# Switch layer of a two-layer ViT tower: 16 experts on every token, against one expert per tile of sorted tokens moved by indirect DMA

## Chip, cores and metric

The program runs on one core of one Trainium2 chip. The metric is the device time of the whole program in microseconds (us), from the first to the last instruction with what lies around it; lower is better. Engines: PE (TensorE, with PEld its weight loads), DVE (VectorE), ACT (ScalarE), POOL (GpSimd), SP (SyncE, which only issues DMAs here).

## What is computed

16 images of 32x32 tokens with 29 features go through two layers, all in float32. S = 1024 tokens of C = 128 features per image.

- Layer 0: tokens are embedded and get a position table; group norm; attention with 8 heads of 64; residual; a causal MLP over features.
- Layer 1: attention with 8 heads of 16, then the switch layer, which is what changes here.

```python
logits = z @ switch_w.T + switch_b                  # z [16, 1024, 128], 16 experts
p, e = max(softmax(logits)), argmax(logits)         # one expert per token
pos = number of earlier tokens (of all images, in order) that chose e
y = z @ expert_w[e].T + expert_b[e]
out = h + (p * y if pos < CAP else p * z)           # CAP = int(1.2 * 16384 / 16)
```

Only one expert's product is used for a token.

## The kernel before

**Order.** Each image passes through segments. In a segment of kind `loop` the core works on three images at once: layer 0 of image i+2 (`seg.l0`), layer 1 of image i+1 (`seg.l1`) and the switch layer of image i (`seg.sw`); the embedding of image i+3 (`seg.nxt`) goes on beside them. The kinds are `first` (layer 0 alone, 208 steps), `second` (both layers, but no switch layer yet), `loop` (13 passes of a hardware loop), `penult` (no embedding) and `final` (layer 1 and a switch layer, 128 steps). `second`, `loop` and `penult` have 256 steps: 32 units (a half of the queries of one head of one layer) of 8 steps, one step for each 128 keys. A layer-0 unit and a layer-1 unit alternate from unit 4 to 27 (`units_of`, L29).

**Steps.** Every engine has its own instruction list, written out by hand in the order of the steps. In a step PE computes one tile of scores (L909 and L911, or L911 alone for layer 1) and one tile of a pass that looks for row maxima (`max_tile`, L883); DVE reduces the latter (L1643), ACT takes the exponential (L1144). Both have two banks, so PE can be two steps ahead. For layer 0 the probabilities are split in two bf16 parts and POOL makes the low part (`lo_parts`, L508), four instructions per unit, at kt 2, 4, 6 and at kt 0 of the next unit. In kt 2, 3, 5, 6 PE multiplies the previous unit's probabilities with the values (L927, L934, or L949 and L959). Row maxima reach the score stacks by a small DMA (`row`, L600): 8 steps before the unit that needs them, 4 steps before it in `final`. SP also loads head stacks (`load_stack`, L603).

**Everything else** is laid between the steps by tables of steps (`switch_slots`, `embed_slots`, `mlp_slots` and others, L141 to 210). A generator on each engine yields the step at which its next piece is due (`Beside`, L306). Such pieces share two PSUM banks, the glue banks, in an order that `glue_plan` (L216) derives from the same tables; `await_filled` and `await_drained` wait on them.

**The switch layer** (`switch`, on PE L827, ACT L1109, POOL L1284, DVE L1558) makes the logits, the one-hot choice `oh` and the rank in its image (`prefix`, added up by POOL, L1292), weights `wgt` and `kr` (0 over capacity), adds `un * z` and the biases to the residual `hm`, and then computes all 16 experts for each of the 8 token tiles: 32 matmuls of 128x512 (L869) against the weights `ewT`, resident in SBUF, in 16 rounds of two, and on DVE 128 multiply-adds (L1633) of a column of `wgt`. Rounds are due at the starts of units 8 to 23 (steps 64 to 185). SP stores `hm` at step 191 (L662). In `final` one switch layer is computed beside the steps, and the last image's follows after them with nothing beside it (prefix `f.`, L1014, L1726): this is called the tail.

## Time and profile before

| | us |
|---|---|
| median of 3 runs (6678.85 to 6692.49) | 6685.7 |
| the profiled execution, its own time | 6688.62 |
| its span in the trace | 6686.8 |
| granted clock of TensorE, mean (1 is 2.4 GHz) | 0.951 |

In the profile an engine's busy time is the time that its instructions cover; `x` is a count. A float32 matmul leaves two records for one instruction; the score tiles, whose type is a rounded float32, leave one. Idle time is put in front of the instruction that ended it, with its releaser. DMAs are listed with the time from issue to landing. The segments begin, by the ACT exponentials that count the steps, at 387.5 (`second`), 743.4 (the loop, about 404 a pass), 5989.6 (`penult`) and 6382.5 (`final`); the last step ends at 6565.

### The profile page before, as it was taken

To read this page: it belongs to the slowest core of one execution; us is meant where nothing else is said; L and a number is where in the kernel's file an instruction comes from. 1 tells how busy PE (TensorE), PEld (TensorE's weight loads), DVE (VectorE), ACT (ScalarE), POOL (GpSimd) and SP (SyncE) were. 2 spreads that over 40 slices of the span, in tenths; PEclk is the share of its full clock that TensorE was granted. 3 is DMA by queue.
4 is the path that set the end of the run, shared out by engine and by line. 5 is a ranking of instruction groups with operands and counts; after the bars stand their busy time and mean duration, and the time that the engine had idled before them with its cause. 6 is when DMAs were issued, how large, how long until landed. Compare 5 with 4: busy or idle time off the path is not lost.

```text
span 6686.8 us, 127962 instructions
## 1 busy us (share of the span) xinstructions
PE 6054.2 (91%) x40167; PEld 4030.8 (60%) x40167; DVE 4525.2 (68%) x11162; ACT 3211.2 (48%) x6321; POOL 2464.2 (37%) x2215
## 2 busy tenths in 40 slices
PE   6889898998989999898998989999899998999986
PEld 4556665666666666665666656666665666666643
DVE  4466676776767767676766767767676676767664
ACT  2345545454455544545445444444455445454541
POOL 2534333433333343333433333333333333333300
PEclk7899999999999999999999999999999999999997
DMA  2131221222122121221211222121221212212110
GB/s 60 42 68 42 59 52 44 52 49 50 42 53 49 40 54 42 60 49 32 64 46 47 49 56 49 40 50 46 55 45 41 61 34 60 52 47 45 30 30 9
DMA packets 98049, 317.05 MB, mean 47 GB/s; under 512 B 27782, under 2 KB 32854, under 8 KB 87126
## 3 DMA queue, kind: packets, MB, share of 16 engines
q1 hardware_dynamic: 97366, 308.41, 19.9%
q8 instruction: 371, 6.08, 0.4%
q14 instruction: 312, 2.56, 0.1%
HBM read 57.19 MB, written 41.94 MB: 15 GB/s over the span
## 4 chain that ended last, share of the span: by engine, by line
issue 47%; POOL 27%; PE 16%; DVE 6%; DMA 1%; POOLq 1%; ACT 1%; SPq 1%; DVEq 0%; ACTq 0%
POOL pr_lo L508 22%; PE bank L883 3%; POOL on L1267 3%; PE bank L911 2%; PE bank L869 2%; DVE mxh L1643 2%; PE bank L949 2%; DVE z L1431 1%; DMA stacks<-parts 1%; PE bank L934 1%; PE bank L927 1%; POOL rs L1238 1%; PE bank L793 1%; PE bank L909 1%; PE bank L959 1%
## 5 line engine op out<-in xcount | busy, mean ns | idle before, releaser
L1643 DVE TENSOR_REDUCE mxh<-bank 128x1 f32<-128x512 f32 x4096 | 2790.7, 687 | 1663.0 <-PE bank L883 1636.9
L1144 ACT ACTIVATE pr<-bank 128x512 f32<-128x512 f32 x4096 | 2419.1, 597 | 2658.8 <-PE bank L911 2613.9
L883 PE MATMUL bank<-stacks 128*128 128x512 f32 x4096 | 2224.3, 544 | 340.9 <-DVE mxh L1643 232.9
L508 POOL TENSOR_TENSOR pr_lo<-pr 128x1024 bf16<-128x1024 f32 x960 | 1823.5, 1900 | 1165.4 <-ACT pr L1144 1165.3
L911 PE MATMUL bank<-stacks 65*128 65x512 f32 (+1 forms) x4096 | 1662.0, 406 | 5.0 <-ACT pr L1144 5.0
L883 PEld LDWEIGHTS bank<-stacks 128*128 128x128 f32 x4096 | 800.8, 196 | 1132.8 <-DVE mxh L1643 809.4
L1267 POOL TENSOR_TENSOR on<-on,o_r 128x128 f32<-128x128 f32 x512 | 235.0, 459 | 1967.6 <-DVE on L1673 1967.5
L911 PEld LDWEIGHTS bank<-stacks 65*128 65x128 f32 (+1 forms) x4096 | 798.7, 195 | 223.6 <-ACT pr L1144 62.0
L909 PE MATMUL bank<-stacks 128*128 128x512 f32 x2048 | 833.5, 407 | 0.2 <-ACT pr L1144 0.2
L869 PE MATMUL bank<-ewT,mx 128*128 128x512 f32 x1024 | 589.0, 662 | 113.9 <-DVE hm L1633 44.8
L927 PE MATMUL bank<-v,pr 128*128 128x129 bf16 x8192 | 654.9, 223 | 0.8 <-ACT pr L1144 0.8
L934 PE MATMUL bank<-v,pr_lo 128*128 128x129 bf16 x8192 | 650.0, 221 | 4.2 <-POOL pr_lo L508 2.5
L927 PEld LDWEIGHTS bank<-v,pr 128*128 128x128 bf16 x8192 | 476.4, 99 | 283.7 <-issue 269.2
L1633 DVE SCALAR_TENSOR_TENSOR hm<-bank,wgt,hm 128x128 f32<-128x128 f32 x2048 | 570.6, 342 | 51.5 <-PE bank L869 51.5
L949 PE MATMUL bank<-pr,v 128*32 128x512 f32 x4096 | 547.0, 609 | 0.0
L934 PEld LDWEIGHTS bank<-v,pr_lo 128*128 128x128 bf16 x8192 | 517.4, 98 | 11.3 <-POOL pr_lo L508 10.3
L909 PEld LDWEIGHTS bank<-stacks 128*128 128x128 f32 x2048 | 403.9, 197 | 132.8 <-ACT pr L1144 77.5
L869 PEld LDWEIGHTS bank<-ewT,mx 128*128 128x128 f32 x1024 | 186.0, 204 | 237.1 <-DVE hm L1633 69.0
L959 PEld LDWEIGHTS bank<-fold,oT 128*128 128x128 f32 x2048 | 267.1, 196 | 59.5 <-ACT oT L1161 46.4
L1044 ACT ACTIVATE parts<-bank,cols 128x512 fp32r<-128x512 f32 x256 | 176.1, 688 | 233.4 <-PE bank L721 232.6
L959 PE MATMUL bank<-fold,oT 128*128 128x32 f32 x2048 | 260.5, 271 | 12.5 <-ACT oT L1161 12.5
L1275 POOL TENSOR_TENSOR on<-on,o_r 128x64 f32<-128x64 f32 x256 | 75.1, 293 | 515.1 <-DVE on L1685 515.0
(171 smaller groups left out, 5072.4 us busy)
## 6 DMA issues: line engine op xcount, KB each, us to landing
stacks<-parts SPq DMA_DIRECT2D x384, 512.0 KB, 6.5
stacks<-parts_d SPq DMA_DIRECT2D x224, 128.0 KB, 3.0
parts_d<-mx SPq DMA_DIRECT2D x16, 1024.0 KB, 4.6
stacks<-parts_d SPq DMA_DIRECT2D x224, 64.0 KB, 2.8
stage<-in_pe SPq DMA_DIRECT2D x16, 512.0 KB, 8.1
stacks<-mrow SPq DMA_DIRECT2D x512, 2.0 KB
parts_d<-on SPq DMA_DIRECT2D x16, 512.0 KB, 5.3
parts_d<-stage SPq DMA_DIRECT2D x16, 512.0 KB, 6.2
```

Of the source, the lines that this page charges most:

```text
L508: return eng.tensor_tensor(low_of(u, kt - 1).rearrange("p a b -> p (a b)"), w, hi, ALU.subtract)
L869: mm(bank[:, :], mT[:, t * P:(t + 1) * P], ewT[:, 4 * q:4 * q + 4, :].rearrange("p e f -> p (e f)"), start=True, stop=True).then_inc(fille ...
L883: mm(maxb[k % 2][:, :], qs[:, t * P:(t + 1) * P], ks[:, g * HALF:(g + 1) * HALF], start=True, stop=True).then_inc(max_filled.sem, 1)
L909: mm(bank[:, :], kA[:, head % 2, kk], qA[:, head % 2, q], start=True, stop=False)
L911: mm(bank[:, :], k_stack(layer, head)[0:last, kk], q_stack(layer, head)[0:last, q], start=(layer == 1), stop=True).then_inc(score_filled.s ...
L927: mm(dst, hi, v0[:, head // 2 % 2, kt, head % 2, 0:w], start=(kt == 0), stop=False)
L934: last = mm(dst, lo, v0[:, head // 2 % 2, kt, head % 2, 0:w], start=False, stop=(kt == T - 1))
L949: last = mm(obank[n % 2][QUAD * r:QUAD * (r + 1), :], v1[:, kt, col:col + QUAD], pr[:, at % 2, kt, :], start=(j == 0), stop=(j == 1))
L959: last = mm(obank[n % 2][:, QUAD * t:QUAD * (t + 1)], oT[:, t * P:(t + 1) * P], fold[:, :], start=True, stop=True)
L1144: act.activation(pr[:, at % 2, kt, :], score[k % 2][:, :], ACT.Exp, scale=SCALES[layer]).then_inc(exp_done.sem, 1)
L1633: ins = dve.scalar_tensor_tensor(hm[:, t, :], bank[:, e * P:(e + 1) * P], wgt[:, t, 4 * q + e:4 * q + e + 1], hm[:, t, :], ALU.mult, ALU.add)
L1643: dve.tensor_reduce(mxh[:, layer, n // 2, n % 2:n % 2 + 1], maxb[k % 2][:, :], AX_X, ALU.max)\
```

## The change

Step 64 to 185's rounds go. In their place:

- DVE builds tables (`tables`, from step 46, 10 instructions and a copy): how many tiles of 128 slots each expert needs in this image, where each expert's slots begin, and the expert of each of 24 tiles. At `place` it adds a slot number per token (4 more instructions).
- POOL scatters the 8 token tiles of `z` by 8 indirect DMAs into `x_sort_d` in DRAM (two a step from step 65), each row at its slot.
- SP loads the sorted tokens in 6 groups of 4 tiles (256 KB each, step 76, then from 86 every 12 steps), reads the expert numbers from SBUF into a register 24 times and loads each tile's 64 KB of weights from `ew_d` in DRAM, two groups ahead, and stores each group's result. In a group the order is: load of the next group, wait for this group's product, four reads and weight loads, store.
- PE transposes 4 tiles (`slots`, step 83 + 12g), ACT moves them, PE multiplies 4 tiles (`product`, 85 + 12g), DVE copies the result out (one step later).
- POOL gathers 8 tiles of results by 8 indirect DMAs (two a step from step 160); DVE adds `kr * y` in 8 instructions (from step 170, after waiting for all gathers). `hm` is stored at step 176.
- In `final` the steps are: `tables` 23, scatter 35, groups from 48 every 10, gather 112, sum 122; in the tail all of it runs in order.
- At the start SP stores the turned weights (1 MB) and three times 512 KB of zeros to DRAM, ahead of the first load of x.

```diff
-        at = {"oT1.0": 1, "oT1.1": 2, "attn1.0": 5, "attn1.1": 6, "ln.0": 7, "ln.1": 8, "z.0": 9, "z.1": 10, "zT3.0": 11, "zT3.1": 13, "logits": 15,
-              "route": 16, "rank": 21, "place": 24, "wT0": 29, "wT1": 30, "eb0": 32, "eb1": 33}
-        first = [37 + 16 * m + s for m in range(6) for s in (0, 3, 8)][:16]
+        at = {"oT1.0": 1, "oT1.1": 2, "attn1.0": 5, "attn1.1": 6, "ln.0": 7, "ln.1": 8, "z.0": 9, "z.1": 10, "zT3.0": 11, "zT3.1": 13,
+              "logits": 15, "route": 16, "rank": 21, "tables": 23, "place": 28, "wT0": 33, "wT1": 34, "eb0": 36, "eb1": 37,
+              "scatter": 35}
+        group, period, sums = 48, 10, (112, 122)
     else:
         at = {"oT1.0": 18, "oT1.1": 19, "attn1.0": 21, "attn1.1": 22, "ln.0": 22, "ln.1": 24, "z.0": 26, "z.1": 28, "zT3.0": 30, "zT3.1": 31,
-              "logits": 36, "route": 38, "rank": 44, "place": 54, "wT0": 59, "wT1": 60, "eb0": 62, "eb1": 63}
-        first = [8 * m for m in range(8, 24)]
-    return {**at, **{f"e{n}.{d}": s + d for n, s in enumerate(first) for d in range(2)}}
-
-
-NO_BANK = ("route", "place", "copy", "res0", "gn", "xn", *(f"{name}.{g}" for name in ("ln", "z", "ln1", "z1", "ln2", "z2") for g in range(2)))
+              "logits": 36, "route": 38, "rank": 44, "tables": 46, "place": 54, "wT0": 59, "wT1": 60, "eb0": 62, "eb1": 63, "scatter": 65}
+        group, period, sums = 80, 12, (160, 170)
+    at.update({f"{name}{g}": group + period * g + step for g in range(GROUPS)
+               for name, step in (("load", 6 - period if g else -4), ("slots", 3), ("product", 5), ("weights", 7), ("store", 7))})
+    return {**at, "gather": sums[0], "sum": sums[1]}
...
+        x_sort, y_sort, y_own = z[:, 0:4, :], z[:, 4:8, :], mT.rearrange("p (t c) -> p t c", t=T)
...
+            def store_prep():
+                sp.dma_start(ew_d.rearrange("e d f -> d e f"), ewT).then_inc(prep_out, 16)
+                for n in range(3):
+                    sp.dma_start(x_sort_d[n * S:(n + 1) * S, :].rearrange("(t p) c -> p t c", p=P),
+                                 stacks1[:, n % 2, 1, :].rearrange("p (t c) -> p t c", t=T).bitcast(F32)).then_inc(prep_out, 16)
...
+            def switch(seg, pre, b):
+                AT = switch_slots(seg.kind)
+                def load_weights(g):
+                    for j in range(4 * g, 4 * g + 4):
+                        e = sp.value_load(tile_ei[0:1, j:j + 1], min_val=0, max_val=E - 1)
+                        sp.dma_start(wring[:, j % 8, :], ew_d[e]).then_inc(weights_in[g % 2].sem, 16)
+                for g in range(2):
+                    yield AT["tables"] + 4 + 2 * g
+                    if g == 0:
+                        await_all((tiles_ready.sem, tiles_ready.at(b, 1)))
+                        sp.nop(nofuse=True)
+                    load_weights(g)
+                def load_slots(g):
+                    sp.dma_start(x_sort, x_sort_d[4 * g * P:4 * (g + 1) * P, :].rearrange("(t p) c -> p t c", p=P))\
+                        .then_inc(x_sort_in.sem, 16)
+                yield AT["load0"]
+                await_all((scattered.sem, scattered.at(b, 16 * T)))
+                load_slots(0)
+                for g in range(GROUPS):
+                    if g + 1 < GROUPS:
+                        yield AT[f"load{g + 1}"]
+                        await_all(drained(seg, f"{pre}slots{g}"))
+                        load_slots(g + 1)
+                    yield AT[f"weights{g}"]
+                    await_all(drained(seg, f"{pre}product{g}"))
+                    if g + 2 < GROUPS:
+                        sp.nop(nofuse=True)
+                        load_weights(g + 2)
+                    yield AT[f"store{g}"]
+                    sp.dma_start(y_sort_d[4 * g * P:4 * (g + 1) * P, :].rearrange("(t p) c -> p t c", p=P), y_sort)\
+                        .then_inc(y_sort_out.sem, 16)
...
-                        await_drained(sp, seg, "e15.1")
+                        await_all((hm_ready.sem, hm_ready.at(seg.sw, 1)))
...
-                for n in range(16):
-                    for d in range(2):
-                        yield AT[f"e{n}.{d}"]
-                        t, q = 2 * (n // 4) + d, n % 4
-                        bank, filled = use(seg, f"{pre}e{n}.{d}")
-                        mm(bank[:, :], mT[:, t * P:(t + 1) * P], ewT[:, 4 * q:4 * q + 4, :].rearrange("p e f -> p (e f)"),
-                           start=True, stop=True).then_inc(filled, 1)
+                for g in range(GROUPS):
+                    yield AT[f"slots{g}"]
+                    te.wait_ge(x_sort_in.sem, x_sort_in.at(b, 16 * (g + 1)))
+                    turn(seg, f"{pre}slots{g}", lambda j: x_sort[:, j, :])
+                    yield AT[f"product{g}"]
+                    te.wait_ge(weights_in[g % 2].sem, weights_in[g % 2].at(b, 64 * (g // 2 + 1)))
+                    bank, filled = use(seg, f"{pre}product{g}", f"{pre}slots{g}")
+                    for j in range(4):
+                        at = g % 2 * HALF + j * P
+                        last = mm(bank[:, j * P:(j + 1) * P], mT[:, at:at + P], wring[:, (4 * g + j) % 8, :], start=True, stop=True)
+                    last.then_inc(filled, 1)
...
+                    if name == "oT0.2.0" and seg.sw:
+                        act.wait_ge(y_sort_out.sem, y_sort_out.at(seg.sw, 16 * GROUPS))
...
+                    move_T(seg, f"{pre}slots{g}", half(mT, g % 2))
...
+                for t in range(T):
+                    if t % 2 == 0:
+                        yield AT["scatter"] + t // 2
+                    if t == 0:
+                        pool.wait_ge(slot_ready.sem, slot_ready.at(b, 1))
+                        pool.nop(nofuse=True)
+                    pool.indirect_dma_start(x_sort_d, bass.IndirectOffsetOnAxis(slot_i[:, t:t + 1], 0), z[:, t, :], None)\
+                        .then_inc(scattered.sem, 16)
+                for t in range(T):
+                    if t % 2 == 0:
+                        yield AT["gather"] + t // 2
+                    if t == 0:
+                        pool.wait_ge(y_sort_out.sem, y_sort_out.at(b, 16 * GROUPS))
+                        pool.nop(nofuse=True)
+                    pool.indirect_dma_start(y_own[:, t, :], None, y_sort_d, bass.IndirectOffsetOnAxis(slot_i[:, t:t + 1], 0))\
+                        .then_inc(y_own_in.sem, 16)
...
-                link(seg, dve.tensor_tensor(prefix[:, 0, :], bank[:, 0:E], seen[:, :], ALU.add))
-                dve.tensor_tensor(seen[:, :], bank[:, E:2 * E], seen[:, :], ALU.add).then_inc(drained, 1)
+                mark(seg, dve.tensor_tensor(prefix[:, 0, :], bank[:, 0:E], seen[:, :], ALU.add))
+                dve.tensor_copy(own, bank[:, E:2 * E]).then_inc(drained, 1)
+                yield AT["tables"]
+                await_drained(dve, seg, f"{pre}rank")
+                over = tile_of[:, 0:T, :].rearrange("p t e -> p (t e)").rearrange("p (e t) -> p e t", t=T)
+                link(seg, dve.tensor_tensor(over, own.unsqueeze(2).broadcast_to([P, E, T]),
+                                            steps_128[:, :].unsqueeze(1).broadcast_to([P, E, T]), ALU.is_gt))
+                link(seg, dve.tensor_reduce(tiles, over, AX_X, ALU.add))
+                yield AT["tables"] + 1
+                below = tile_of[:, 0:E, :]
+                link(seg, dve.tensor_tensor(below, tiles.unsqueeze(1).broadcast_to([P, E, E]), earlier[:, :, :], ALU.mult))
+                link(seg, dve.tensor_reduce(begin, below, AX_X, ALU.add))
+                yield AT["tables"] + 2
+                mark(seg, dve.tensor_tensor(tiles, tiles, begin, ALU.add))
+                link(seg, dve.scalar_tensor_tensor(shift, begin, float(P), seen[:, :], ALU.mult, ALU.subtract))
+                mark(seg, dve.tensor_tensor(seen[:, :], own, seen[:, :], ALU.add))
+                link(seg, dve.tensor_tensor(tile_of[:, :, :], tiles.unsqueeze(1).broadcast_to([P, TILES, E]),
+                                            tile_no[:, :].unsqueeze(2).broadcast_to([P, TILES, E]), ALU.is_le))
+                yield AT["tables"] + 3
+                link(seg, dve.tensor_reduce(tile_e[:, :], tile_of[:, :, :], AX_X, ALU.add))
+                dve.tensor_scalar(tile_ei[:, :], tile_e[:, :], float(E - 1), None, ALU.min).then_inc(tiles_ready.sem, 1)
...
+                yield AT["place"] + 2
+                link(seg, dve.tensor_tensor(lg[:, :, :], oh[:, :, :], shift.unsqueeze(1).broadcast_to([P, T, E]), ALU.mult))
+                link(seg, dve.tensor_reduce(slot[:, :], lg[:, :, :], AX_X, ALU.add))
+                link(seg, dve.tensor_tensor(slot[:, :], slot[:, :], pos, ALU.add))
+                mark(seg, dve.tensor_copy(slot_i[:, :], slot[:, :]))
                 for t in range(T):
                     if t % 4 == 0:
-                        yield AT["place"] + 2 + t // 4
+                        yield AT["place"] + 3 + t // 4
                     ins = dve.scalar_tensor_tensor(hm[:, t, :], z[:, t, :], un[:, t:t + 1], hm[:, t, :], ALU.mult, ALU.add)
-                    if t % 4 == 3:
+                    if t == 3:
                         mark(seg, ins)
-                settle(seg)
+                link(seg, ins)
+                dve.sem_inc(slot_ready.sem, 1)
                 for g in range(2):
                     yield AT[f"eb{g}"]
                     add_result(seg, f"{pre}eb{g}", g, hm, hm)
-
-                for n in range(16):
-                    yield AT[f"e{n}.1"] + 1
-                    if n == 0:
+                for g in range(GROUPS):
+                    yield AT[f"product{g}"] + 1
+                    bank, drained = await_filled(dve, seg, f"{pre}product{g}")
+                    if g > 0:
+                        dve.wait_ge(y_sort_out.sem, y_sort_out.at(b, 16 * g))
+                    dve.tensor_copy(y_sort, bank_tiles(bank)).then_inc(drained, 1)
+                for t in range(T):
+                    if t % 2 == 0:
+                        yield AT["sum"] + t // 2
+                    if t == 0:
+                        dve.wait_ge(y_own_in.sem, y_own_in.at(b, 16 * T))
                         await_drained(dve, seg, f"{pre}eb0", f"{pre}eb1")
-                    elif n % 4 > 0:
-                        await_drained(dve, seg, f"{pre}e{n - 1}.0", f"{pre}e{n - 1}.1")
-                    both = [await_filled(dve, seg, f"{pre}e{n}.{d}") for d in range(2)]
-                    q = n % 4
-                    for e in range(4):
-                        if e == 2:
-                            yield AT[f"e{n}.1"] + 2
-                        for d, (bank, drained) in enumerate(both):
-                            t = 2 * (n // 4) + d
-                            if e > 0:
-                                settle(seg, 0 if (e, d) == (3, 1) else 1)
-                            ins = dve.scalar_tensor_tensor(hm[:, t, :], bank[:, e * P:(e + 1) * P],
-                                                           wgt[:, t, 4 * q + e:4 * q + e + 1], hm[:, t, :], ALU.mult, ALU.add)
-                            if e == 3:
-                                ins.then_inc(drained, 1)
-                            else:
-                                mark(seg, ins)
+                    ins = dve.scalar_tensor_tensor(hm[:, t, :], y_own[:, t, :], kr[:, t:t + 1], hm[:, t, :], ALU.mult, ALU.add)
+                ins.then_inc(hm_ready.sem, 1)
...
-STORE_STEPS = {"loop": 191, "penult": 191, "final": 124}
+STORE_STEPS = {"loop": 176, "penult": 176, "final": 126}
```

## Rows read from the trace of the kernel before

**Rows 1.** The profile's page: span, busy time of each engine.
```profile
...
span 6686.8 us, 127962 instructions
...
PE 6054.2 (91%) x40167; PEld 4030.8 (60%) x40167; DVE 4525.2 (68%) x11162; ACT 3211.2 (48%) x6321; POOL 2464.2 (37%) x2215
...
```

**Rows 2.** Busy us of each engine in five stretches (window, length, engines, clock, DMA).
```profile
core 0: us, PE busy (x) PEld busy (x) DVE busy (x) ACT busy (x) POOL busy (x), PEclk, DMA share, GB/s
482.71:639.47 156.76, 150.62 (x1109) 100.67 (x1107) 102.48 (x222) 88.06 (x183) 71.27 (x61) 1.00 0.24 55
627.04:639.47 12.43, 10.93 (x61) 6.77 (x60) 11.14 (x37) 5.61 (x13) 8.40 (x8) 1.00 0.11 32
3272.61:3459.29 186.68, 179.15 (x1173) 115.29 (x1172) 135.91 (x353) 88.55 (x182) 70.34 (x59) 0.97 0.22 49
3439.11:3459.29 20.18, 16.85 (x65) 9.50 (x64) 12.79 (x47) 5.67 (x13) 8.54 (x8) 0.75 0.14 47
6095.52:6271.08 175.56, 172.24 (x1146) 110.95 (x1145) 130.38 (x328) 87.03 (x179) 67.86 (x55) 0.99 0.21 49
```

**Rows 3.** Groups of the stretch 3272.61 to 3459.29, by line.
```profile
...
L1643 DVE TENSOR_REDUCE mxh<-bank 128x1 f32<-128x512 f32 x128 | 88.1, 688 | 45.5 <-PE bank L883 45.0
...
L508 POOL TENSOR_TENSOR pr_lo<-pr 128x1024 bf16<-128x1024 f32 x32 | 60.7, 1898 | 40.4 <-ACT pr L1144 40.4
...
L1633 DVE SCALAR_TENSOR_TENSOR hm<-bank,wgt,hm 128x128 f32<-128x128 f32 x128 | 35.7, 342 | 0.0
L869 PE MATMUL bank<-ewT,mx 128*128 128x512 f32 x64 | 35.4, 636 | 5.1 <-DVE parts L1443 1.9 <-DVE stage L1438 1.7 <-DVE v L1455 1.1
...
```

**Rows 4.** Timeline of PE, three places: start, length, what.
```profile
...
2102.77 1.02 PE L869 MATMUL bank<-ewT,mx 128*128 128x512 f32 x2
...
2103.86 0.40 PE L911 MATMUL bank<-stacks 128*128 128x512 f32 x1
...
2120.28 0.64 PE L710 MATMUL bank<-tri_sb,on 128*128 128x128 f32 x4
...
2120.99 0.40 PE L909 MATMUL bank<-stacks 128*128 128x512 f32 x1
...
3370.60 1.11 PE L728 MATMUL bank<-wv_sb,xnT 128*128 128x128 f32 x8
...
3371.78 0.39 PE L911 MATMUL bank<-stacks 128*128 128x512 f32 x1
```

**Rows 5.** SP's DMA instructions of line 600, ns min/median/max.
```profile
...
L600 SPq DMA_DIRECT2D stacks<-mrow x512: 572/635/680, 81.7 to 6555.2; - x171
...
```

**Rows 6.** DMA issues by line: KB each, median us to landing.
```profile
...
stacks<-parts_d SPq DMA_DIRECT2D x224, 64.0 KB, 2.8
...
out<-hm SPq DMA_DIRECT2D x16, 512.0 KB, 2.7
...
```

**Rows 7.** Timeline of POOL, one instruction.
```profile
...
3456.38 2.04 POOL L508 TENSOR_TENSOR pr_lo<-pr 128x1024 bf16<-128x1024 f32 x1
```

**Rows 8.** Two stretches of the final segment, columns as in rows 2.
```profile
6404.08:6412.62 8.54, 8.09 (x46) 4.17 (x45) 7.86 (x23) 5.24 (x11) 0.69 (x4) 1.00 0.10 24
6422.91:6557.87 134.96, 114.82 (x526) 57.60 (x526) 91.50 (x244) 56.75 (x112) 3.51 (x12) 0.97 0.06 16
```

**Rows 9.** Timeline of all engines, the tail.
```profile
...
6590.73 0.29 DVE L1601 TENSOR_TENSOR lg<-oh,prefix 128x128 f32<-128x128 f32 x1 [2.10 <-POOL prefix L1292]
...
6597.64 3.63 PE L869 MATMUL bank<-ewT,mx 128*128 128x512 f32 x4
...
6601.40 2.16 DVE L1633 SCALAR_TENSOR_TENSOR hm<-bank,wgt,hm 128x128 f32<-128x128 f32 x8 [2.97 <-PE bank L869]
...
6683.75 0.36 SPq L665 DMA_DIRECT2D out<-hm  x1
```

**Rows 10.** Timeline of all engines, the start.
```profile
...
35.00 0.37 SPq L565 DMA_DIRECT2D xin<-in_x  x1
...
37.14 1.88 PE L710 MATMUL bank<-tri_sb,xin 128*29 128x128 f32 x8 [8.46 <-DMA xin<-in_x]
...
```

More of the change, by code:

```diff
@@ L11 @@
 BF16 = mybir.dt.bfloat16
+U32 = mybir.dt.uint32
 ALU = mybir.AluOpType
@@ L26 @@
 LEAD = 4
+TILES, GROUPS = 24, 6
 def units_of(kind):
@@ L652, in segment @@
                     load_x(seg.nxt)
+                if seg.kind == "second":
+                    sp.wait_ge(prep_out, 64)
+                beside = [Beside(switch(seg, "", seg.sw))] if seg.sw else []
                 for step in range(LAST[seg.kind]):
@@ L659, in segment @@
                         load_positions(seg, seg.nxt)
+                    for work in beside:
+                        work.run(step)
                     if seg.sw and step == STORE_STEPS[seg.kind]:
-                        await_drained(sp, seg, "e15.1")
+                        await_all((hm_ready.sem, hm_ready.at(seg.sw, 1)))
                         sp.dma_start(out_v[seg.sw.index()], hm[:, :, :]).then_inc(out_stored.sem, 16)
                 if seg.kind == "final":
-                    await_drained(sp, seg, "f.e15.1")
+                    Beside(switch(seg, "f.", seg.l1)).run(LAST_STEP)
+                    await_all((hm_ready.sem, hm_ready.at(seg.l1, 1)))
                     sp.dma_start(out_v[seg.l1.index()], hm[:, :, :]).then_inc(out_stored.sem, 16)
@@ L1126, in switch @@
                     move_T(seg, f"{pre}wT{g}", xT[0:E, g * HALF:(g + 1) * HALF], E)
+                for g in range(GROUPS):
+                    yield AT[f"slots{g}"]
+                    move_T(seg, f"{pre}slots{g}", half(mT, g % 2))
             def max_rows(seg, name, b, layer, head, g):
@@ L1372, in _ @@
             dve.memset(seen[:, :], 0.0)
-            dve.wait_ge(prep_dve, 2)
+            for n in range(T):
+                dve.memset(steps_128[:, n:n + 1], float(P * n))
+            for n in range(TILES):
+                dve.memset(tile_no[:, n:n + 1], float(n))
+            dve.memset(earlier[:, :, :], 0.0).then_inc(prep_dve, 1)
+            dve.wait_ge(prep_dve, 3)
+            for n in range(1, E):
+                dve.memset(earlier[:, n, 0:n], 1.0)
             dve.memset(v1_heads[:, :, :, D1:D1 + 1], 1.0)
@@ L1574, in switch @@
                 top, total, rp, vm, pos, kr, un = (small[:, n, :] for n in range(7))
+                own, tiles, begin, shift = (counts[:, n, :] for n in range(4))
                 yield AT["logits"]
```

37 lines of the change are left out of this document (32 added, 5 removed).

## Prediction

> **What bounds the kernel now.** I read the page first: PE is busy 91% of the span, no other engine over 68% [rows 1]. Busy shares don't say what a removed instruction is worth, so I went on to busy time by stretch. The kernel holds its own comparison: segment `second` runs the same 128 steps 64 to 191 as a pass of the loop, without a switch layer. Without it they take 156.76 us, with it, in the seventh pass, 186.68 [rows 2]. In both PE is busy 96%, so it is the bound in either case, and 29.9 us a pass is the most that taking the experts away can give. Of these, 7.75 lie in the last unit, 20.18 against 12.43, where expert rounds and the embedding push each other about and the granted clock falls to 0.75, against 1.00 without experts [rows 2]. The groups by line show what goes: 64 PE records and 128 DVE instructions [rows 3]. The timeline of PE gives the price at full clock. From the start of an expert instruction to the second tile after it pass 1.09 us, of which 0.23 is the max tile between: 0.86 us each, 27.5 for 32 [rows 4]. Work and loss agree.
>
> **Part by part, for a pass.**
> *Removed:* the whole 29.9 us; the 35.7 us of DVE [rows 3] lay beside PE and are in that figure where they didn't.
> *PE added:* six groups. Four transposes and one max tile take 0.71 us, so 0.48 without the tile; four float32 products of 128 columns and one tile 1.18, so 0.95 [rows 4]. 6 x 1.43 = 8.6 us, all on the path, since PE is 96% busy without them.
> *DVE added:* six copies of 0.69 (the reduction of the same 128x512 bank [rows 3]), eight sums at 0.27 (2.16 us for 8 [rows 9]), 14 small table instructions at about 0.3 (0.29 for 128 elements [rows 9]; the widest have three times that). Some 10 us against 35.7 removed, hidden by PE but for the tables: 4 us in four steps of about 1.3, where DVE has its reductions too. I count 1.5 on the path. *ACT added:* six moves, 88 of 157 us busy [rows 2], hidden.
> *SP added:* 24 reads, 24 weight loads, 12 loads and stores. An issue is 0.64 us [rows 5], so without the reads 23 us in 400, hidden by SP's idle time. A register read isn't in the trace; nearest rows: 0.64 (an issue, below which it may fall to nearly nothing) and 2.7 (a whole DMA, issue to landing [rows 6]). I take 0.7, near the issue, as it also is a thing of SP alone. Behind these stand the row DMAs. Four reads and loads take 5.4 us. In group 0 they start at step 86 + 0.9 us (PSUM copied) and end, with the store, 6.9 us after step 86; the row due at step 88 goes out some 4.5 us after its step. A step lasts 1.22 us (156.76 / 128). The row's slack is 8 steps, 9.8 us, less 1 for transpose and move, 0.6 issue and 2.8 landing [rows 5, 6]: 5.4. Hidden, with 1 us to spare; in `final`, with 4 steps, not.
> The Trainium skill ("DMA: Bandwidth & Descriptors", Latency and other measured facts) gives `tensor_load` a floor of about 600 ns; no row here shows one. If that is this read, its price would be 0.6 and the sum the same within 1 us.
> *POOL added:* 16 indirect DMAs. No row shows one. Bounds: 0.6 (SP's issue [rows 5]) and 1.9 (POOL's costliest instruction, pr_lo [rows 3]), and above it if each row's address is written by software. I take 1.2, the middle: more work than an issue, no data moved. The gather is due at step 160, behind a pr_lo: 1.9 + 8 x 1.2 + 2.7 landing = 14.2 us, and DVE waits for it at step 170, 12.2 us later. Stall: 2.0 us, all on the path, since DVE's reductions then stand still and PE has two banks. The scatter: POOL is free for pr_lo at 1.9 + 9.6 + 0.8 = 12.3 us after step 65, pr_lo is due 9 steps (11.0) later; the 1.3 us are made up, for four pr_lo take 7.6 of the unit's 9.8 us. Sorted tokens are there 1.9 + 9.6 + 2.7 + 0.6 + 2.8 = 17.6 us after step 65, PE wants them after 18 steps, 22 us. Hidden.
> *DMA:* 4 MB more a pass, where the DMA engines are busy 0.22 of the stretch [rows 2]. 64 KB land in 2.8 us, 512 KB in 2.7 [rows 6]; two groups ahead they are hidden. 1 us for collisions.
> Sum: 29.9 - 8.6 - 1.5 - 2.0 - 1.0 = 16.8 us a pass, **218 in 13 passes**.
>
> **The other segments.** `penult` has no embedding, and its stretch is 175.56 us long [rows 2]. What experts cost outside the last unit is 29.9 - 7.75 = 22.1; less 13.1: **-9**. `final`: steps 32 to 126 take 134.96 us, a unit without rounds 8.54 [rows 8]. At that pace 11.9 units are 102, a loss of 33 to the rounds. Back come 8.6 of PE, about 3 x 3.5 for rows whose 4 steps of slack (4.3 us) SP's reads eat up, 2 for the gather: **-12**. The tail: experts start at 6597.64 and all ends at 6683.75, 86.1 us [rows 9]. New: tables end at about 6592.5 (place now starts at 6590.73 [rows 9], waiting for POOL, which hides half of them), slots at 6597, scatter 9.6 + 2.7 to 6609. Groups: SP binds, with 0.6 load, 5.4 reads and weight loads, 0.6 store and the wait for the product, 7.3 for each of four; the last two, a chain of load 3.4, transposes, move, product, copy 5, 8.2 each: 46, to 6655. Store 2.7, gather 9.6 + 2.7, sums 2.2: 6672. **-12**. The start: x is issued at 35.00 and used at 37.14 [rows 10]; ahead of it stand now five times 512 KB, 2.7 us each if alone [rows 6]: 0 to 13.5, since in part they run beside each other. **+8**.
> Sum: -218 - 9 - 12 - 12 + 8 = -243. The profiled execution took 6688.6, 3 over the median of 6685.7; against the median 6443.
>
> **Rivals.**
> *A, indirect DMAs are dear (slower).* Let one take c on POOL. Gather stall 8c - 7.6 (1.9 + 2.7 - 12.2), scatter 8c - 9.5 in pr_lo: 16c - 17.1. It eats the 29.9 - 8.6 - 1.5 - 1.0 = 18.8 at **c = 2.25 us**; PE then waits at L934 and DVE at its sum. At c = 2.7 a pass loses 7.3, 14 of them 102, the tail gains 1.5 x 16 = 24 over its -12, the start 8, `final` 5: 6686 + 127 = 6813. Against it: pr_lo, with 1024 elements a partition, takes 1.9 [rows 3]. For it: addresses of 128 rows each. 10%. POOL's pr_lo is 1.90 as a rule, but 2.04 at 3456.38, beside DVE's work [rows 3, 7]. The Trainium skill ("DMA: Bandwidth & Descriptors", SWDGE vs HWDGE vs iDMA) says that the descriptor rings are SBUF state out of which DVE locks GpSimd in its 2-port mode: by that rule c would grow with DVE's load, toward this rival. The trace shows only that 7%, and I leave c at 1.2.
> *B, SP's reads are dear.* At 2 us a read, four loads take 10.6; rows of steps 88 and 112 come some 4 us late, those of 104 and 128 as well, and the next store reaches DVE's copy late: 4 x 4 us a pass eat all but 1; with the tail 20 later, about 6680. Against: 0.64 for the whole issue. 6%.
> *C, in between:* c near 1.7. Gather 6.0, scatter 4.1 in place of 2.0: 8 a pass less, 112, tail and `final` 11: 6565. 16%.
> *D, all cheap:* c = 0.7, no stall, no collision: 19.8 x 13, penult 12, final 20, tail 25, start 3: 6375. For it: the steps between scatter, load and sum. 15%.
> *E, no relief:* another engine takes PE's place at once. Excluded by the 156.76 of `second` [rows 2], but for POOL, which is A.
>
> **Numbers.** The forecast's own case has 53%, range 6400 to 6520. 0.2%, 13 us, is about what can be told from no change. Range for 8 in 10: from D into C, 6360 to 6590, leaving out A, B and edges. Faster: forecast 53, C 16, D 15, half of B: 87%. Same: 3%. Slower: A, 10%.
>
> **What would show it.** In the loop, steps 64 to 191 at about 170 us with PE busy over 95%; the last unit near 12.4 at clock 1.00; L869 and L1633 gone. Indirect DMAs about 1.2 us apart, DVE idle some 2 us before the first sum. SP's row DMAs on time in the loop, late in `final`. The tail's groups about 7.5 us apart. I am wrong if PE waits at L934 for pr_lo (A), at L911 for rows (B), or if the stretch stays over 180 with neither.

## The result, and the profile after

| | before | after |
|---|---|---|
| median of 4 runs each | 6682.27 us | 6590.88 us (6576.14 to 6603.23) |
| the profiled execution / its span | 6688.62 / 6686.8 | 6587.05 / 6585.3 |
| granted clock, mean | 0.951 | 0.934 |

The ratio is 0.9859, 95% interval 0.9842 to 0.9876: 91 us less, where 243 were forecast. Lines have moved: the max tile L883 is L969, L911 is L997, the reduction L1643 is L1778, pr_lo L508 is L541, the product with pr_lo L934 is L1020, the adds of `un*z` L1610 are L1752, the exponential L1144 is L1236. New are the tables (the first of their instructions is L1720), the scatters (L1394), the gathers (L1402), the sums `hm + kr * y` (L1772) and SP's register reads (L686). "Unit n" is steps 8n to 8n+7.

From the page of after:

```profile
span 6585.3 us, 128361 instructions
...
PE 5849.4 (89%) x40295; PEld 4041.3 (61%) x40295; DVE 4245.7 (64%) x9610; ACT 3267.1 (50%) x6417; POOL 2719.6 (41%) x2471
...
L997 PE MATMUL bank<-stacks 65*128 65x512 f32 (+1 forms) x4096 | 1695.6, 414 | 12.0 <-DMA stacks<-mrow 6.7
```

PE has lost 205 us of busy time, the span 101: half of what PE gained has come back as idle time. In the last row, rows of maxima delay PE by 6.7 us in the whole program, all of it in `final` (four waits, from 6361.6 on), so in the loop SP's reads are not it. The windows of after, with the columns of [rows 2]: `second` (steps 64 to 191), then of the seventh pass unit 6, units 7 and 8, steps 64 to 191, unit 20, unit 21, unit 23.

```profile
491.05:650.32 159.27, 153.53 (x1109) 101.82 (x1107) 102.42 (x222) 88.06 (x182) 71.31 (x61) 0.98 0.24 54
3230.58:3243.73 13.15, 11.25 (x95) 7.99 (x94) 10.71 (x26) 6.68 (x16) 4.54 (x10) 1.00 0.11 31
3243.73:3271.37 27.64, 24.85 (x164) 17.64 (x164) 19.76 (x43) 12.14 (x26) 16.15 (x15) 0.88 0.33 75
3261.36:3434.38 173.02, 163.45 (x1181) 113.67 (x1180) 112.51 (x236) 91.84 (x188) 84.72 (x74) 0.96 0.34 83
3385.09:3393.65 8.56, 8.48 (x84) 6.39 (x83) 5.64 (x11) 5.04 (x12) 6.97 (x8) 1.00 0.66 152
3393.65:3411.13 17.48, 13.96 (x58) 9.10 (x58) 11.92 (x22) 6.61 (x14) 10.65 (x10) 0.74 0.21 48
3421.82:3434.38 12.56, 10.93 (x61) 6.75 (x60) 11.19 (x37) 5.64 (x13) 8.46 (x8) 1.00 0.11 33
```

Two places stand out. Unit 21 takes 17.48 us at a clock of 0.74; without a switch layer, in `second`, it takes 10.3. Units 6 and 7 lie ahead of the stretch that the forecast looked at: over 13 passes (taken from the starts of the ACT exponentials) unit 6 goes from 10.78 to 13.17 us and unit 7 from 15.07 to 18.63. The timeline of DVE, PE and POOL shows the first:

```profile
3396.23 0.95 POOL L1402 DMA_INDIRECT mx<-y_sort_d,slot_i  x1 [0.30 <-issue]
3397.91 3.73 POOL L541 TENSOR_TENSOR pr_lo<-pr 128x1024 bf16<-128x1024 f32 x2
3399.47 2.59 DVE L1772 SCALAR_TENSOR_TENSOR hm<-mx,small,hm 128x128 f32<-128x128 f32 x2 [3.39 <-DMA mx<-y_sort_d,slot_i]
3401.99 0.68 DVE L1778 TENSOR_REDUCE mxh<-bank 128x1 f32<-128x512 f32 x1
3402.59 0.60 DVE L1772 SCALAR_TENSOR_TENSOR hm<-mx,small,hm 128x128 f32<-128x128 f32 x2
3402.72 0.80 PE L969 MATMUL bank<-stacks 128*128 128x512 f32 x1 [3.11 <-DVE mxh L1778]
...
3405.03 2.24 DVE L1772 SCALAR_TENSOR_TENSOR hm<-mx,small,hm 128x128 f32<-128x128 f32 x2
3405.08 2.04 POOL L541 TENSOR_TENSOR pr_lo<-pr 128x1024 bf16<-128x1024 f32 x1 [3.44 <-ACT pr L1236]
```

DVE waits 3.39 us for the gathers. Then its first two sums take 2.59 us instead of 0.60: they end 0.4 us after POOL's two pr_lo (3397.91 + 3.73 = 3401.64). The first of the two takes 2.33 us of this: it begins during one pr_lo, at 3399.47, and is held through the whole of the next as well. The same again at 3405.03, ending just behind the pr_lo at 3407.12. PE has stood still for 3.11 us, and its tile now takes 0.80 instead of 0.50: the granted clock, 1.00 until then, is 0.50 (1.2 GHz instead of 2.4) from 3402.1 to 3412.4. In unit 7 it is the adds of `un*z`, which the change has moved by one step:

```profile
3247.52 1.89 POOL L541 TENSOR_TENSOR pr_lo<-pr 128x1024 bf16<-128x1024 f32 x1 [2.75 <-ACT pr L1236]
3248.15 2.20 DVE L1752 SCALAR_TENSOR_TENSOR hm<-z,small,hm 128x128 f32<-128x128 f32 x4
3250.14 1.96 POOL L541 TENSOR_TENSOR pr_lo<-pr 128x1024 bf16<-128x1024 f32 x1 [0.73 <-ACT pr L1236]
3250.87 2.16 DVE L1752 SCALAR_TENSOR_TENSOR hm<-z,small,hm 128x128 f32<-128x128 f32 x4
3254.01 0.50 PE L969 MATMUL bank<-stacks 128*128 128x512 f32 x1 [1.60 <-DVE mxh L1778]
```

Both groups of four meet a pr_lo (2.20 and 2.16 us for four whose median is 0.34 each); before the change one group took 1.13 and the other 2.08. A table instruction just ahead of unit 6 meets one as well (L1720, median 0.86 us, least 0.28):

```profile
3227.59 1.89 POOL L541 TENSOR_TENSOR pr_lo<-pr 128x1024 bf16<-128x1024 f32 x1 [2.00 <-ACT pr L1236]
3228.77 0.86 DVE L1720 TENSOR_TENSOR tile_of<-counts,steps 128x128 f32<-128x128 f32 x1
```

POOL's and SP's new instructions cost what was forecast, or less. The groups of POOL's instructions, and the register read on SP:

```profile
L1394 POOL DMA_INDIRECT x_sort_d<-z,slot_i x128 | 125.6, 981 | 45.8 <-issue 36.8 <-DVEq L1756 9.0
L1402 POOL DMA_INDIRECT mx<-y_sort_d,slot_i x128 | 122.1, 954 | 85.7 <-DMA y_sort_d<-z 49.0 <-issue 34.5
```

```profile
L686 SPq TENSOR_LOAD <-tile_ei x384: 262/273/1272, 839.8 to 6555.9; - x192
L686 SPq FUSED_REGOPS  x384: 147/152/186, 840.3 to 6556.2; - x192
```

An indirect DMA is 0.95 us and 0.30 until the next: c = 1.25. A read is 0.27 + 0.15.

### The profile page after: what moved, and what is told of

Read it like the earlier page. It is cut to its first block, busy times and chain, and to the rows that moved or that the text cites. A ratio compares the mean times of both kernels' runs of the same rounds, so it can differ in the third digit from the quotient of the medians.

```text
span 6585.3 us, 128361 instructions
## 1 busy us (share of the span) xinstructions
PE 5849.4 (89%) x40295; PEld 4041.3 (61%) x40295; DVE 4245.7 (64%) x9610; ACT 3267.1 (50%) x6417; POOL 2719.6 (41%) x2471
## 4 chain that ended last, share of the span: by engine, by line
issue 45%; POOL 30%; PE 15%; DVE 6%; DMA 2%; SPq 1%; ACT 1%; POOLq 1%; DVEq 0%; ACTq 0%
POOL pr_lo L541 22%; PE bank L969 3%; POOL on L1360 3%; PE bank L997 2%; DVE mxh L1778 2%; POOL x_sort_d L1394 1%; POOL mx L1402 1%; PE bank L1035 1%; DMA stacks<-parts 1%; DVE z L1547 1%; PE bank L1020 1%; PE bank L1013 1%; PE bank L875 1%; POOL rs L1331 1%; PE bank L995 1%
## 5 line engine op out<-in xcount | busy, mean ns | idle before, releaser
L1778 DVE TENSOR_REDUCE mxh<-bank 128x1 f32<-128x512 f32 x4096 | 2776.1, 687 | 1713.2 <-PE bank L969 1688.3
L1236 ACT ACTIVATE pr<-bank 128x512 f32<-128x512 f32 x4096 | 2424.8, 597 | 2460.0 <-PE bank L997 2405.3
L969 PE MATMUL bank<-stacks 128*128 128x512 f32 x4096 | 2101.2, 514 | 486.9 <-DVE mxh L1778 372.9
L541 POOL TENSOR_TENSOR pr_lo<-pr 128x1024 bf16<-128x1024 f32 x960 | 1822.5, 1900 | 1027.1 <-ACT pr L1236 1026.9
L997 PE MATMUL bank<-stacks 65*128 65x512 f32 (+1 forms) x4096 | 1695.6, 414 | 12.0 <-DMA stacks<-mrow 6.7
L969 PEld LDWEIGHTS bank<-stacks 128*128 128x128 f32 x4096 | 814.8, 199 | 1255.4 <-DVE mxh L1778 966.1
L997 PEld LDWEIGHTS bank<-stacks 65*128 65x128 f32 (+1 forms) x4096 | 816.5, 199 | 177.9 <-ACT pr L1236 33.6
L995 PE MATMUL bank<-stacks 128*128 128x512 f32 x2048 | 842.1, 411 | 0.2 <-ACT pr L1236 0.2
L1020 PE MATMUL bank<-v,pr_lo 128*128 128x129 bf16 x8192 | 659.7, 222 | 6.5 <-POOL pr_lo L541 2.5
L1020 PEld LDWEIGHTS bank<-v,pr_lo 128*128 128x128 bf16 x8192 | 522.5, 99 | 18.3 <-POOL pr_lo L541 16.6
L995 PEld LDWEIGHTS bank<-stacks 128*128 128x128 f32 x2048 | 407.9, 199 | 70.3 <-ACT pr L1236 33.9
L1045 PEld LDWEIGHTS bank<-fold,oT 128*128 128x128 f32 x2048 | 288.3, 209 | 61.4 <-ACT oT L1253 45.2
L1045 PE MATMUL bank<-fold,oT 128*128 128x32 f32 x2048 | 279.6, 283 | 12.5 <-ACT oT L1253 12.5
L1807 DVE RECIPROCAL o_r<-bank 128x2 f32<-128x2 f32 x512 | 87.4, 171 | 253.5 <-ACT o_hi L1245 252.2
L1114 ACT ACTIVATE mx<-bank 128x512 f32<-128x512 f32 (+1 forms) x256 | 152.4, 596 | 183.4 <-PE bank L792 183.4
L1035 PEld LDWEIGHTS bank<-pr,v 128*32 128x32 f32 x4096 | 81.7, 109 | 198.0 <-issue 181.1
```

The costliest lines, as they stand in the source:

```text
L541: return eng.tensor_tensor(low_of(u, kt - 1).rearrange("p a b -> p (a b)"), w, hi, ALU.subtract)
L969: mm(maxb[k % 2][:, :], qs[:, t * P:(t + 1) * P], ks[:, g * HALF:(g + 1) * HALF], start=True, stop=True).then_inc(max_filled.sem, 1)
L995: mm(bank[:, :], kA[:, head % 2, kk], qA[:, head % 2, q], start=True, stop=False)
L997: mm(bank[:, :], k_stack(layer, head)[0:last, kk], q_stack(layer, head)[0:last, q], start=(layer == 1), stop=True).then_inc(score_filled.s ...
L1020: last = mm(dst, lo, v0[:, head // 2 % 2, kt, head % 2, 0:w], start=False, stop=(kt == T - 1))
L1035: last = mm(obank[n % 2][QUAD * r:QUAD * (r + 1), :], v1[:, kt, col:col + QUAD], pr[:, at % 2, kt, :], start=(j == 0), stop=(j == 1))
```

## The experiments

18 runs were made on six chips, called chip 1 to chip 6 in their order; each was used once, for all the runs of its group. Whether the first measurement of the change was on one of them is not on record. The kernel before ran beside them on each and takes the same on all (medians 6680 to 6692).

**Chip 1: the two theories, and a surprise.** Theory 1: the gather's stall. Theory 2: DVE work pushed into pr_lo's time.

```diff
-        group, period, sums = 80, 12, (160, 170)
+        group, period, sums = 80, 12, (160, 177)
-STORE_STEPS = {"loop": 176, "penult": 176,
+STORE_STEPS = {"loop": 183, "penult": 183,
```

> The eight sums at step 177 instead of 170, the store of hm at 183 instead of 176; all else as after the change. Theory 1 (the gathers' wait at step 170, and the sums run beside pr_lo): unit 21 of a pass falls from 17.4 us to about 10.3, its length without experts, so 7 us a pass less, 14 passes: about 6495. Rival 1 (the unit is long because of what the groups and the gathers do to DMA or PE, whoever waits): unit 21 keeps 14 us or more, total over 6550. In between (a half of the wait moves to step 177): 6530.

With 173 and 179 in place of 177 and 183:

> The eight sums at step 173, when the last gather has landed, but still beside pr_lo; store at 179. If the wait is what costs (3.4 us of idle DVE and then half clock), nearly all of the 7 us comes back: 6500. If the sums' being held beside pr_lo costs by itself, the four pairs still last about 2.4 us in place of 0.6 where they meet it, PE waits and the clock falls: unit 21 about 14, total 6540 to 6560.

```diff
-                yield AT["place"] + 2
-                link(seg, dve.tensor_tensor(lg[:, :, :], oh[:, :, :], shift.unsqueeze(1).broadcast_to([P, T, E]), ALU.mult))
...
                 for t in range(T):
                     if t % 4 == 0:
-                        yield AT["place"] + 3 + t // 4
+                        yield AT["place"] + 2 + t // 4
...
+                yield AT["place"] + 5
+                link(seg, dve.tensor_tensor(lg[:, :, :], oh[:, :, :], shift.unsqueeze(1).broadcast_to([P, T, E]), ALU.mult))
...
```

> The adds of un*z to hm go back to the steps that they had before the change (place + 2 and + 3), the four slot instructions follow them at place + 5. Theory 2 (one step's shift put both groups of adds beside pr_lo): one of the two groups of four falls from 2.2 to 1.1 us, PE's idle 1.6 us and the low clock of units 7 and 8 go: units 6 to 8 fall from 41.5 to about 38 us, total 6545. Rival 2 (units 6 to 8 are long because DVE has tables and slots to do at all): unchanged within 1 us a pass, 6580 to 6600.

> Both edits, sums at step 177 and adds of un*z ahead of the slots. If theories 1 and 2 hold and their places don't touch, the gains add: 6591 - 96 - 45 = 6450. If one clock state or one wait holds both, less: the better of the two alone plus at most a third of the other.

Measured: 6667.04, 6714.25, 6684.20 and 6641.35 us, ratios 0.9977 (0.9964 to 0.9989), 1.0047, 1.0006 and 0.9939. All expectations failed: every kernel was slower than the change without an edit had been in its first measurement (it did not run on chip 1). In all four, unit 8 had become 3 to 4 us longer and unit 20 6 us, though one edit touched neither.

**Chips 2 and 3: the change itself, again.**

> The changed kernel once more, nothing edited: the four edits all show a stretch of some 4 to 6 us at steps 65 to 67 and 165 in which no semaphore of PE moves, while indirect DMAs run; the first measurement of the changed kernel has none there. If the stretches belong to the edits (the place of code or of a transfer): 6580 to 6605 again, units 20 and 8 at 8.6 and 9.7 us. If they belong to the chip or to the day: units 20 and 8 at about 14.7 and 13.5 us, total near 6690, and all four edits are to be compared with this run.

6603.74 us, ratio 0.9871 (0.9848 to 0.9893), units 8 and 20 as at first. On chip 3, beside three edits:

> The changed kernel unedited, on the same chip as the three below: 6590 to 6605 if the chip is like the one of the first measurement; near 6690 with units 8 and 20 at 13.5 and 14.7 us if PE's long stretches without a semaphore belong to a chip.

6688.02 us in 10 runs (6677.49 to 6695.55), ratio 1.0006 (0.9996 to 1.0017). **The same program gains 91 and 80 us in two measurements and nothing in a third.** Its timeline there, unit 20 of the seventh pass (DVE, ACT, PE and POOL):

```profile
3429.24 0.69 DVE L1778 TENSOR_REDUCE mxh<-bank 128x1 f32<-128x512 f32 x1 [0.84 <-PE bank L969]
3430.55 0.47 PE L969 MATMUL bank<-stacks 128*128 128x512 f32 x1
3431.03 0.95 POOL L1402 DMA_INDIRECT mx<-y_sort_d,slot_i  x1 [0.30 <-issue]
3432.00 0.47 PE L969 MATMUL bank<-stacks 128*128 128x512 f32 x1
3434.78 0.95 POOL L1402 DMA_INDIRECT mx<-y_sort_d,slot_i  x1 [0.30 <-issue]
3435.81 0.69 DVE L1778 TENSOR_REDUCE mxh<-bank 128x1 f32<-128x512 f32 x1 [4.39 <-remote]
3435.85 0.60 ACT L1236 ACTIVATE pr<-bank 128x512 f32<-128x512 f32 x1 [5.21 <-remote]
3436.56 0.80 PE L969 MATMUL bank<-stacks 128*128 128x512 f32 x1 [3.85 <-issue]
```

DVE and ACT stand still for 4.39 and 5.21 us, while PE goes on until its banks are full and POOL keeps its 1.25 us. The semaphore events of the trace say what they wait for (start of a matmul that signals, then when its signal is recorded):

```
signal of      matmul starts at       signal recorded at
L969 (DVE)     3430.55                3435.79
L997 (ACT)     3430.87                3435.82
L1020          3431.97                3438.74
L969 (DVE)     3432.00                3438.77
L997 (ACT)     3432.31                3438.81
```

Otherwise a signal comes 0.4 to 0.6 us after the start; these come 5.0 to 6.8 after it, the last three 0.034 us apart. The traces of all eight runs on chips 1 and 3 show this at steps 164 and 65 to 69 of every pass, always while eight indirect DMAs run; in the first measurement and on chips 2, 4, 5 and 6 none does. I call it the hold.

The record has holes in these stretches: signals of DVE and ACT that fell due at 3430.6 to 3431.4 stand nowhere in it, though PE took at 3432.00 a bank that DVE had just drained. Of the 4097 signals of the max reductions this trace records 4038, that of the first measurement all. The hold itself is seen without the record, by the late starts of DVE and ACT; whether the signal or the end of the matmul is late is not shown, since a trace gives only a matmul's start directly.

The three beside it:

> Sums at step 177, store of hm at 183, as once before. If PE's stretches without a semaphore at steps 65 and 164 belong to the chip, not the edit, they are gone where the run beside it has none, and theory 1 gives 7 us a pass less than that run: 6495 to 6510. If they belong to this edit: 6665 again.

> Sums at 177 and the adds of un*z back at steps 56 and 57, as once before, where it took 26 us less than the sums alone. If the stretches belong to the chip: 25 us under the run of the sums alone, 6470 to 6485. If to the edit: 6640 again.

```diff
-"tables": 46
+"tables": 49
```

> As the one before, with the tables from step 49 instead of 46, so that none of their instructions meets a pr_lo. Theory 2a (the meeting costs: 0.86 us in place of 0.27 twice): unit 6 falls from 13.2 us by about 1, 13 us in all. Rival (it is DVE's sheer work of 4 us in one unit): unit 6 stays within 0.4 us or grows.

Measured 6654.85, 6637.22 and 6599.39 us; each edit pays on top of the one before (33, 18 and 38 us). The adds of `un*z` shorten unit 7 by 1.2 us. The last edit beat its expectation: unit 6 falls from 13.16 to 10.76 us, so all that the tables had cost it is gone (2.40, expected 1), and unit 7 by another 0.95, though DVE does the same work. For unit 6 the rival (sheer work) is refuted. Unit 7 is now 16.56 us, 1.5 more than before the change; no run says why.

**Chip 4, without the hold.**

> The best version so far (sums at 177, adds of un*z at 56 and 57, tables at 49) once more, as the reference of the two below on this chip. 6600 if this chip holds PE's semaphores back while indirect DMAs run (unit 20 at 14.7 us), 6455 to 6480 if it doesn't (unit 20 at 8.6 us).

> The reference with the sums back at step 170 and the store at 176, as in the change. Theory 1: slower than the reference by 5 to 7 us a pass (70 to 100 us) on a chip that doesn't hold PE's semaphores back; by 1.5 to 2.5 a pass (20 to 35) on one that does, since there the hold at step 164 delays PE by itself and the gathers land meanwhile. Rival (the sums' place is worth nothing): within 10 us of the reference on either.

6424.10 us (6413.42 to 6437.30), ratio 0.9608 (0.9582 to 0.9634), and 6502.37. The sums' place is worth 78 us, 5.6 a pass: theory 1 holds. Against the unedited change on chip 2, also without the hold, the kernel with the sums at 170 has units 6 and 7 shorter by 2.42 and 2.93 us and takes 101 less in all (88 less than in the first measurement, where unit 7 of the unedited change is itself 1.0 shorter): theory 2.

```diff
-                    if t % 2 == 0:
-                        yield AT["gather"] + t // 2
+                    yield AT["gather"] + (t // 2 if seg.kind == "final" else 2 * t)
```

with the same for the scatter, groups from 88 instead of 80, sums at 179:

> The reference with one indirect DMA every second step (scatter from 65 to 79, gather from 160 to 174) instead of eight in a row, the groups 8 steps later, the sums at 179, the store at 187. Theory 3 (a row of indirect DMAs 1.25 us apart is what holds PE's semaphores back for 5 us; one alone holds them for less than the two steps that the banks give): units 8 and 20 lose their 4 and 6 us, 14 passes at about 9: 6475 on such a chip, and 6450 to 6480, as the reference, on the other. Rival 3 (each single one holds them for some 3 us or more): no gain, or slower than the reference, since now eight steps are hit instead of two.

6512.18 us, 88 slower than its reference, against the expectation. Over half of it is seen in its timeline: a scatter at step 79 falls between two pr_lo, the next is late, and PE waits for it at L1020 for 3.06 us (POOL and PE):

```profile
3634.42 1.01 POOL L1393 DMA_INDIRECT x_sort_d<-z,slot_i  x1 [0.17 <-issue]
3635.46 1.90 POOL L541 TENSOR_TENSOR pr_lo<-pr 128x1024 bf16<-128x1024 f32 x1
3637.42 0.40 PE L1020 MATMUL bank<-v,pr_lo 128*128 128x129 bf16 x2 [3.06 <-POOL pr_lo L541]
```

Unit 10 grows by 3.69 us, and unit 22 by 1.33, of 7.0 a pass. On the hold it says nothing, as there was none.

**Chip 5, without the hold.**

> The reference (sums at 177, adds of un*z at 56 and 57, tables at 49) on the chip of the three below: 6424 if the chip doesn't hold PE's semaphores back, 6599 if it does.

> The reference with the sums at step 173 and the store at 179: the gathers have landed, but the sums still meet two pr_lo. If the sums' slowness beside pr_lo is a cost of its own, slower than the reference by 2 to 4 us a pass (30 to 55 us, of the 78 that sums at 170 cost); if the wait is all, within 10 us of the reference. This holds on either kind of chip.

6421.46 and 6468.27 us. With the sums at 173, POOL and DVE:

```profile
3342.09 5.59 POOL L541 TENSOR_TENSOR pr_lo<-pr 128x1024 bf16<-128x1024 f32 x3
```

```profile
3344.76 0.16 DVE L1783 TENSOR_REDUCE mx<-mxh 128x4 f32<-128x8 f32 x1
3345.03 3.07 DVE L1772 SCALAR_TENSOR_TENSOR hm<-mx,small,hm 128x128 f32<-128x128 f32 x2
3348.62 0.60 DVE L1772 SCALAR_TENSOR_TENSOR hm<-mx,small,hm 128x128 f32<-128x128 f32 x2
```

No wait for the gathers is left, yet two sums take 3.07 us and end 0.4 after the last of three pr_lo (3347.68). That alone costs 47 us, 3.3 a pass, as the first case of the expectation had it; the other 31 of the 78 are the wait.

> The reference with four indirect gathers instead of eight (half of the tokens get no result of their expert); the scatter is whole. On a chip that holds PE's semaphores back: if the hold begins some 2.6 us after the first gather and lasts as long as a row of them goes on, unit 20 falls from 14.7 us to about 9.5, unit 8 stays: 65 us less. If it is the first one or two that do it, unit 20 stays at 14 or more. On the other kind of chip: within 5 us of the reference, since the gathers stand beside other work.

> The reference with one gather every second step from 160 to 174, the sums at 179, the store at 187; scatter and groups unchanged. On a chip that holds PE's semaphores back: theory 3 (close succession does it) unit 20 falls to 8.6 us while unit 8 stays at 13.5, about 80 us less; rival 3 (each one does it) units 20 and 21 together stay at 26 or more. On the other kind: 1.3 us a pass slower, as the last sums then wait for the last gather.

6416.51 us with half of the gathers (5 less than its reference), 6443.26 with the gathers spread, 22 more: unit 22 is 1.33 longer, as expected. The windows of the reference: unit 6, units 7 and 8, steps 64 to 191, units 20, 21, 23.

```profile
3157.07:3167.82 10.75, 10.75 (x95) 7.72 (x93) 10.14 (x25) 6.57 (x16) 3.90 (x9) 1.00 0.03 8
3167.82:3193.24 25.42, 23.21 (x164) 16.14 (x164) 19.35 (x44) 12.02 (x26) 14.93 (x14) 0.93 0.37 82
3184.41:3349.52 165.11, 159.13 (x1181) 109.34 (x1180) 109.29 (x236) 91.25 (x187) 85.03 (x75) 0.98 0.36 87
3306.83:3315.38 8.55, 8.47 (x84) 6.40 (x83) 5.63 (x11) 5.05 (x13) 6.97 (x8) 1.00 0.66 153
3315.38:3325.76 10.38, 9.96 (x58) 6.04 (x58) 6.30 (x14) 6.17 (x14) 9.61 (x10) 1.00 0.35 80
3335.97:3349.52 13.55, 12.37 (x61) 7.05 (x60) 11.09 (x37) 5.57 (x12) 8.49 (x8) 0.87 0.10 31
```

**Chip 6, without the hold again.**

> One gather every second step from 160 to 174, sums at 179, store at 187, the rest as the reference, once more. On a chip that holds PE's semaphores back: theory 3 (close succession does it) unit 20 at 8.6 us while unit 8 is at 13.5; rival 3 (each one does it) units 20 and 21 together at 26 or more. On the other kind 6443 again.

6445.50 us; the question of theory 3 was not put.

```diff
-            store_prep()
...
                     load_x(seg.l0)
                     load_positions(seg, seg.l0)
+                    store_prep()
```

> The reference with the stores of the turned weights and of the zeros behind the first loads of x and of the position table instead of ahead of them. If these five transfers are what makes the start 8 us longer, the first exponential comes at 85.1 us instead of 93: 8 us less than the reference. If their traffic or ACT's wait for them (it mustn't overwrite the weights before they are out) counts, 89 or more.

6413.55 us, ratio 0.9603 (0.9584 to 0.9622); the first exponential at 84.1 us instead of 92 to 93. The start of after, and of this:

```profile
34.17 5.34 SPq L594 DMA_DIRECT2D x_sort_d<-stacks  x3
39.55 1.82 SPq L606 DMA_DIRECT2D xin<-in_x  x1
45.26 1.88 PE L792 MATMUL bank<-tri_sb,xin 128*29 128x128 f32 x8 [16.81 <-DMA xin<-in_x]
```

```profile
33.88 0.37 SPq L605 DMA_DIRECT2D xin<-in_x  x1
35.99 1.88 PE L792 MATMUL bank<-tri_sb,xin 128*29 128x128 f32 x8 [8.43 <-DMA xin<-in_x]
```

On chip 6 this kernel is 271 us under the kernel before (0.9603); the change was 91 under it in its first measurement (0.9859). The reference did not run on chip 6, so that the stores cost the start its 8 us rests on the first exponential and not on the total.

## Why the prediction was wrong in size

The sign held, and so did the way by which PE is relieved. But 91 us came instead of 243, and the median, 6590.88, lies at the upper edge of the range (6360 to 6590), just beyond it. Two terms of the sum were far too small, the gather's stall and the tables, and behind most of both stands what the forecast had no term for: DVE's sums of two SBUF operands held up by POOL's pr_lo. The total came near rival C's 6565, but not by C's cause, a dearer indirect DMA.

- **Removed, 29.9 a pass:** held but for 2.5. `second` itself, whose code is unchanged, takes 159.27 for these steps instead of 156.76 (its unit 23 runs at a lower clock). Why is open; in the traces of all 19 runs with the change unit 23 of `second` has a clock of 0.77 or 0.87 and takes 13.4 to 15.0 us, against 12.43 at 1.00 before.
- **PE's groups, 8.6, and DMA collisions, 1.0:** steps 64 to 191 take 166.0 us a pass in the reference on chip 5, where the stalls are gone, and `second` 159.2 there: 6.8 for both, on the mean. The 4 MB that the forecast gave the DMAs are too few: scatter and gather move 0.5 MB each, the loads, weights and stores 1.5 each, 5.5 in all.
- **c = 1.2:** 1.25. Rivals A (2.25 and more), C (1.7) and D (0.7) are out by it, and A's DVE load doesn't show: 954 to 1207 ns over 128 scatters. The rule of the Trainium skill ("DMA: Bandwidth & Descriptors", SWDGE vs HWDGE vs iDMA), by which DVE in its 2-port mode locks GpSimd out of its descriptor rings, didn't raise c here; whether DVE was ever in that mode beside a scatter no run shows.
- **SP's read, 0.7:** 0.43, rows on time in the loop. In `final` they were late, as forecast: 6.7 us of waits, where 3 x 3.5 were counted. `final` came out at -22 instead of -12; the rows explain 4 of these 10 us, the rest is open.
- **Gather stall, 2.0, failed: 7.1 a pass.** The step in the prediction is "Stall: 2.0 us, all on the path". The landing was forecast well, 14.2 us after step 160 begins, and comes at 14.4 (3399.47); but step 170 begins after 10.8 us and not after 12.2, since the steps from 160 on take 1.08 us where the forecast used the mean of a stretch, 1.22 [rows 2]. So the wait was 3.4. To it come the sums that POOL's pr_lo holds up, and half the clock behind PE's standstill: unit 21 takes 17.4 us instead of 10.3. Moving the sums away gave back 5.6 a pass. The forecast priced eight sums at 0.27 from the tail [rows 9], where POOL does nothing.
- **Tables on DVE, 1.5, failed: 6 a pass.** It is "4 us in four steps of about 1.3, where DVE has its reductions too"; unit 6 +2.4, unit 7 +3.6. Of these 6, moving the tables took back 2.4 and 0.95, and moving the adds of `un*z`, which the change had shifted by one step and so both beside pr_lo, 1.2: mostly not the work costs but the meeting with pr_lo. The other 1.5 stay open. The forecast read the stretch from step 64 on, and this lies ahead of it.
- **penult:** -2.8 instead of -9; it runs the same steps, but no run took its terms apart. **Tail:** -15 instead of -12 (107.2 us for 122.4 from the last exponential on). Its groups come 7.9 us apart, where 7.3 were forecast, but that is luck: the reads are cheaper than forecast, and the landing of each store, 2.7 us, for which DVE's next copy waits, stands in no term of the four. **Start:** +8.1, forecast 8, and shown by the last experiment.

A pass, before to after: -29.9 + 2.5 (`second`'s own) + 7.1 (gather) + 7.5 (what is left in steps 64 to 191, the groups above all) = -12.8, near the measured 186.9 to 173.9; steps outside +7.4, of which units 6 and 7 are 6.0. Together -5.6, x 13 = -73; with -3, -22, -15, +8 and `second`'s +5 some -100, the difference of the two profiled executions (101.6). With the three edits a pass takes 385.4 us, 18.2 less than before and near the 16.8 forecast. That agreement is partly luck, as the forecast counted steps 64 to 191 alone, and there it is 20.8.

The Trainium skill ("SBUF — State Buffer", SBUF: two separate sides) says that a DVE instruction with two SBUF inputs and a GpSimd instruction that reads SBUF exclude each other for their whole length. The traces agree: each held sum ends 0.15 to 0.16 us after a pr_lo, reductions out of PSUM are not held (0.68 beside it), and the experts' multiply-adds before [rows 3], with one input in PSUM, weren't either (342 ns on the mean, 354 at most). They show one thing more: where two pr_lo follow each other, a sum that begins during the first waits for the second too.

What stays open: the hold. Shown is that the same program has it in one measurement and not in two others, that it comes only while indirect DMAs run, and that PE goes on starting matmuls until its banks are full while DVE and ACT, which wait for its signals, stand still. As no chip was used twice, it may go with the chip or with what else differed that time (its host, the day). Whether fewer or wider spaced ones avoid it was asked in three kernels, which met no such chip.

## What to carry to other kernels

When work moves from PSUM operands to SBUF operands, look up for each new DVE instruction what POOL does in that step: an SBUF-SBUF sum that takes 0.34 us alone takes up to 2.9 beside long POOL instructions that follow each other, and an engine two banks ahead can't hide it. Place such instructions by POOL's timetable, and read also the steps ahead of the stretch that a change is about. Where a kernel uses indirect DMAs beside PE, measure it on several chips before trusting a gain of a few per cent.
